# Layer 0's cross-attention attends with still values and sums by ones; the rotation of layer 1's keys goes from GpSimd to VectorE

## The chip, the cores and the metric

One core of one Trainium2 chip runs the whole program in a single launch. A core has TensorE (matrix products, 128 x 128, results to PSUM), VectorE (DVE), ScalarE (ACT), GpSimd (POOL) and SyncE (SP, which issues DMAs). The engines run side by side and meet only at semaphores; each runs its own instructions in order. Times are device microseconds (us) of the core; the metric is the median time of an execution.

## The reference

A decoder of four layers, each with self-attention, cross-attention to a context and a feed-forward part, every one followed by a residual and a layer norm. x has 16 blocks of 128 tokens and 256 features, the context as many. All arithmetic is f32. What matters here is the second of the twelve parts, layer 0's cross-attention (12 heads of 64):

```python
kv_in = layernorm(tab_x, tab_g, tab_b)
q = layernorm(layernorm(x, vid_g, vid_b) @ Wq, q_g, q_b)
k = layernorm(kv_in @ Wk, k_g, k_b)
v = kv_in @ Wv
q, k, v = (split(q) * scale, split(k), split(v))      # 12 heads of 64
sim = jnp.einsum('bhid,bhjd->bhij', q, k)
attn = jax.nn.softmax(sim, axis=-1)
out = jnp.einsum('bhij,bhjd->bhid', attn, v)
out = out.transpose(0, 2, 1, 3).reshape(x.shape[0], x.shape[1], INNER)
return out @ Wo + bo
```

and, from layer 1's cross-attention, the rotation of the keys, which the kernel makes two stages earlier than it needs them, in the stage of layer 1's self-attention (a gated convolution):

```python
k = proj(key, Wk, bk, Lk)
k = apply_rope(k, k_cos, k_sin)     # [x1 * c - x2 * s, x1 * s + x2 * c]
```

## The kernel before

The program is a chain of stages. Within a stage every engine has a list of instructions written out by hand, and waits on counting semaphores; between stages all engines meet.

**Layer 0's cross-attention** (`l0_xattn`) treats the 16 blocks in 16 turns. All 768 = 12 x 64 inner features of a block are held as two halves of 384, six heads each; a head pair (j = 0, 1) lies on the lower and upper 64 partitions. A turn n does the scores and the attention of block n, the projections of block n + 1, the input norms of blocks n + 2 and n + 3, and the output of block n - 1. In a turn TensorE does, in this order: scores for the row maxima (`scores(1)`, `scores(0)`, L1245), the transposes of block n - 1's attended rows (`turn_out`, L1236), the query projection (L1230), the turned maxima (L1251), input transposes (L1224), output projection of block n - 1 (L1280), the scores again, turned so that the keys lie on partitions, with the maxima subtracted by a product (L1258, L1261), the key projection (L1230), the transposes of the normalised queries `qn`, the attend products (L1270), the transposes of block n - 1's result into `XT` (`turn_back`, L1286), those of the normalised keys `kn`, and the value projection.

The attend product of a head takes the exponentials `Pr` (keys on partitions, queries as columns) as weights and streams the values, 64 columns and one column of ones that makes the sum of the row. So the result has queries on partitions, and a row's sum is one number on its partition. VectorE then inverts 12 sums (`rinv`, L1476), multiplies (`on`, L1479), and TensorE must transpose `on` six times and ScalarE copy it (`oT`, L1388) before the output projection can use it.

VectorE's order in a turn: two `maximum` (L1471), moments and normalisation of the next block's queries (`wide_moments`, `wide`), input moments, residual and norm of block n - 1, moments and normalisation of the next keys (`wide(n + 1, 1)`, L1456, giving `kn`), `normalise(n)`, and `keys(n + 1)` (L1463), which scales the six transposed key tiles into `kT`, first the three of half 1, then those of half 0; the next turn's `scores` wait for these. The result of a turn's attend products lies in `pS[0]`, which `scores(0)` of the next turn overwrites.

Nobody reads the `XT` that this stage writes: the feed-forward stage behind it starts from `X` and writes `XT` anew.

**Layer 1's convolution stage** (`l1_attn`) treats the tokens in four groups of 512. Per group and per quarter m of the 512 inner features: TensorE projects (L1898), ScalarE stores (`inputs`, L1949) and makes the first tap, VectorE adds three taps (`convolve`, L2009), ScalarE applies SiLU (L1963); TensorE makes the gates (L1908), ScalarE their sigmoid (L1970), VectorE the product `yT` (`products`, L2021), TensorE the output (L1922), and VectorE and GpSimd the norm (`tail`). Beside it the keys of layer 1 (`core.keys1`, 2 x 2048 elements per partition) are rotated in four chunks of 1024: VectorE swaps partners by a shuffle (`turn_keys`, L2025, two chunks ahead of group 0, one between groups 0 and 1, one behind group 1), and GpSimd multiplies by the cosines, multiplies the swapped ones by the sines, and adds (L1877 to L1879).

Of the kernel before, what the change touches and what calls it, by code (L numbers as in the profile page):

```python
# [16 lines left out]
P = 128  # L17
NB = 16
# [1034 lines left out]
def l0_xattn(core, a):  # L1053
# [6 lines left out]
    VX = DHX + 1  # L1060
    LAST = NB - 1
    with Stage(core, "x0") as s:
# [16 lines left out]
        qn, kn, on = (s.sb(n, [P, INNER]) for n in ("qn", "kn", "on"))  # L1079
        qT, kT, oT = (s.sb(n, [P, KI, P]) for n in ("qT", "kT", "oT"))  # L1080
        V = s.sb("V", [P, H, VX])
# [5 lines left out]
        rinv = s.sb("rinv", [P, 2, H // 2])  # L1087
# [4 lines left out]
        pO = pS[0]  # L1092
        pI = pS[1][:, 0, :].rearrange("p (k n) -> p k n", k=2 * KD)
        pX = pS[1][:, 1, 0:D].rearrange("p (k n) -> p k n", k=KD)
        y = pT[:, 0, 0:D]

        CLEARED = 5
# [17 lines left out]
        o_ready, o_inverted, on_ready = s.sem("o_ready"), s.sem("o_inverted"), s.sem("on_ready")  # L1115
        onT_ready, oT_stored = s.sem("onT_ready"), s.sem("oT_stored")
# [3 lines left out]
        xT_ready, xT_stored = s.sem("xT_ready"), s.sem("xT_stored")  # L1120
# [96 lines left out]
        def _(pe):  # L1217
# [59 lines left out]
            def output(b):  # L1277
                pe.wait_ge(oT_stored, b + 1)
# [3 lines left out]

            def turn_back(b):
                pe.wait_ge(xn_ready, b + 1)
                for k in range(KD):
                    ins = pe.transpose(pX[:, k, :], xn[:, bass.ts(k, P)], core.ident[:])  # L1286
                ins.then_inc(xT_ready, 1)
# [3399 lines left out]
```

## Time and profile before

| | |
|---|---|
| median of 3 runs | 2604.66 us (2603.99 to 2605.37) |
| the profiled execution's own time | 2604.75 us |
| its span, first to last instruction | 2602.9 us |
| granted TensorE clock, mean over the span | 0.947 |
| layer 0's cross-attention, about | 141 to 488 us |
| layer 1's convolution stage, about | 592 to 726 us |

The page of the profile gives busy times by engine, the timeline gives single instructions or runs of equal ones with their start and length, the windows give busy shares and granted clock of stretches. PE is TensorE's matrix products, PEld its weight loads. One f32 product shows as two passes of PE in such rows. The granted clock is a share of 2.4 GHz; 0.50 is 1.2 GHz. Names are those of the program with a letter for the stage (x_ for a cross-attention, a_ for layer 1's convolution stage).

### The profile page before, as it was taken

The numbers are of one execution on the slowest core, as the hardware profiler recorded it, in microseconds if no ns is written. First come the engines' busy times: TensorE is split into PE (matmuls) and PEld (weight loads), VectorE is DVE, ScalarE is ACT, GpSimd is POOL, SyncE is SP. The second block draws the span as 40 slices with busy tenths as digits, with TensorE's granted clock in tenths as the row PEclk, the third lists the DMA queues.
The fourth block names the chain that finished last, engine by engine and source line by source line (L and its number), as shares of the span: only waits on it lengthen the run. The fifth ranks groups of instructions, "written<-read, shape, count | busy, mean of one in ns | idle before, by whom it ended". The sixth has DMA issues, their size and how long they took to land. (4 is left out here: it accounts for less than half of the span.)

```text
span 2602.9 us, 48661 instructions
## 1 busy us (share of the span) xinstructions
PE 2283.5 (88%) x18360; PEld 1789.3 (69%) x18369; DVE 1313.6 (50%) x2768; ACT 908.1 (35%) x1591; POOL 708.3 (27%) x1096
## 2 busy tenths in 40 slices
PE   8869999787989999999979988977976889599992
PEld 4647777453567465899968866735865768399992
DVE  4566666698668421111167755553147787511114
ACT  2233333484346301111122225522225667122223
POOL 1722222235223100222212211211324532133332
PEclk9889999898989999999999989988988999799996
DMA  7500000100020100788610002013620000399994
GB/s 282 187 1 1 0 0 1 26 2 0 1 92 2 52 0 1 295 315 315 232 49 0 0 25 73 2 51 89 180 62 5 2 2 3 108 325 326 324 327 138
DMA packets 162729, 253.57 MB, mean 97 GB/s; under 512 B 17296, under 2 KB 123537, under 8 KB 162321
## 3 DMA queue, kind: packets, MB, share of 16 engines
q1 hardware_dynamic: 153360, 230.42, 25.7%
q0 software_dynamic: 9216, 21.06, 3.0%
q8 instruction: 103, 1.69, 0.3%
q14 instruction: 50, 0.40, 0.1%
HBM read 219.79 MB, written 31.13 MB: 96 GB/s over the span
## 5 line engine op out<-in xcount | busy, mean ns | idle before, releaser
L3510 PE MATMUL te_pU<-te_xsT,te_wu 128*128 128x128 f32 x1952 | 233.7, 277 | 1.5 <-DVE te_xsT L3603 1.5
L3510 PEld LDWEIGHTS te_pU<-te_xsT,te_wu 128*128 128x128 f32 x1952 | 231.3, 193 | 5.2 <-issue 2.1
L3531 PE MATMUL te_pY<-te_wd,te_hT 128*128 128x256 f32 x976 | 220.8, 379 | 0.0
L3531 PEld LDWEIGHTS te_pY<-te_wd,te_hT 128*128 128x128 f32 x976 | 180.7, 190 | 22.0
L1230 PE MATMUL x_pB<-early,x_xlT 128*128 128x384 f32 x376 | 133.4, 499 | 1.7 <-ACT x_xlT L1362 1.7
L3560 ACT ACTIVATE te_hT<-te_pU 128x512 f32<-128x512 f32 x78 | 46.6, 597 | 235.0 <-PE te_pU L3510 235.0
L2541 DVE TENSOR_REDUCE x_mx<-x_pR 128x8 f32<-128x1024 f32 x64 | 78.3, 1223 | 78.0 <-PE x_pR L2301 78.0
L3584 DVE COPY te_ys<-te_pY 128x256 f32<-128x256 f32 x61 | 25.9, 425 | 162.8 <-PE te_pY L3531 162.8
L3579 DVE TENSOR_TENSOR te_hT<-te_pU,te_sg 128x512 f32<-128x512 f32 x44 | 30.4, 692 | 147.5 <-ACT te_sg L3558 147.5
L2541 DVE TENSOR_REDUCE a_mx<-a_pR 128x8 f32<-128x1024 f32 x64 | 78.3, 1224 | 44.2 <-PE a_pR L2301 44.2
L3558 ACT ACTIVATE te_sg<-te_pG 128x512 f32<-128x512 f32 x44 | 26.3, 597 | 210.2 <-PE te_pG L3510 210.2
L1230 PEld LDWEIGHTS x_pB<-early,x_xlT 128*128 128x128 f32 x376 | 68.8, 193 | 43.1 <-issue 4.3
L2301 PE MATMUL a_pR<-a_kx,a_qx 32*128 32x128 f32 x1024 | 74.7, 282 | 24.7 <-DVE a_qx L2548 18.6
L2445 ACT ACTIVATE x_Pr<-x_pT 128x1024 f32<-128x1024 f32 x64 | 65.6, 1025 | 79.8 <-PE x_pT L2306 79.8
L3581 DVE COPY te_xsT<-te_pT 128x256 f32<-128x256 f32 x61 | 25.7, 421 | 130.8 <-PE te_pT L3504 130.8
L2301 PEld LDWEIGHTS a_pR<-a_kx,a_qx 32*128 32x128 f32 x1024 | 63.4, 186 | 38.1 <-issue 23.9
L3472 POOL COPY te_home<-moe_home 128x1 uint32 (+1 forms) x61 | 11.1, 181 | 286.7 <-DVE te_ys L3584 286.7
L3510 PE MATMUL te_pG<-te_xsT,te_wg 128*128 128x128 f32 x704 | 85.8, 275 | 0.0
L2301 PEld LDWEIGHTS x_pR<-x_kx,x_qx 32*128 32x128 f32 x1024 | 66.5, 196 | 25.0 <-issue 21.7
L2301 PE MATMUL x_pR<-x_kx,x_qx 32*128 32x128 f32 x1024 | 79.0, 294 | 4.3 <-DVE x_qx L2548 3.7
L3510 PEld LDWEIGHTS te_pG<-te_xsT,te_wg 128*128 128x128 f32 x704 | 82.1, 192 | 0.0
L3462 POOL DMA_INDIRECT te_xs<-xs_slots,te_token x65 | 64.9, 998 | 51.9 <-POOL te_token L3459 51.9
(669 smaller groups left out, 5624.8 us busy)
## 6 DMA issues: line engine op xcount, KB each, us to landing
te_wu<-in_L_ffn_w_upT SPq DMA_DIRECT2D x39, 1024.0 KB, 5.9
te_wd<-in_L_ffn_w_downT SPq DMA_DIRECT2D x39, 1024.0 KB, 5.8
te_wu<-in_L_ffn_up SPq DMA_DIRECT2D x22, 1024.0 KB, 4.9
te_wg<-in_L_ffn_gate SPq DMA_DIRECT2D x22, 1024.0 KB, 6.9
te_wd<-in_L_ffn_down SPq DMA_DIRECT2D x22, 1024.0 KB, 7.6
moe_first<-in_L_ffn_W SPq DMA_DIRECT2D x8, 1024.0 KB, 8.5
xs_slots<-zeros SPq DMA_DIRECT2D x1, 5120.0 KB, 15.6
ys_slots<-zeros SPq DMA_DIRECT2D x1, 5120.0 KB, 28.9
```

The costliest lines, as they stand in the source:

```text
L1230: ins = pe.matmul(to[:, n, 0:HALF], xlT[t][:, src + k, :], w[:, k, bass.ts(n, HALF)], start=(k == 0), stop=(k == KD - 1))
L2301: return pe.matmul(pR[:, j, c, :], qx[b % 4][g, c, :], kx[b % 4][g, c, :], start=mask is None, stop=mask is None or c == SLOTS16 - 1)
L2445: ins = act.activation(Pr[b % 2][half][:], pT[:], ACT.Exp, scale=SCALE)
L2541: dve.tensor_reduce(out, pR[:].rearrange("p j (i t) n -> p (j i) t n", i=PAIR), AX.X, ALU.max).then_inc(mx_ready[half], 1)
L3462: pool.indirect_dma_start(xs[u][:], None, core.XS, bass.IndirectOffsetOnAxis(token[u][:, 0:1], 0)).then_inc(x_loaded[u], 16)
L3510: ins = pe.matmul(out[g][:, m, :], w[:, k, bass.ts(PER * g + m, P)], xsT[:, k, :], start=(k == 0), stop=(k == KD - 1))
L3531: ins = pe.matmul(pY[u][:, 0, :], hT[:, k, :], wd[u][:, k, :], start=(k == 0), stop=(k == KH - 1))
L3558: act.activation(sg[g][:], pG[g][:], act_fn).then_inc(g_done, 1)
L3560: act.activation(hT[:, PER * g:PER * (g + 1), :], pU[g][:], act_fn).then_inc(h_done, 1)
L3579: dve.tensor_tensor(hT[:, PER * g:PER * (g + 1), :], pU[g][:], sg[g][:], ALU.mult).then_inc(h_done, 1)
L3581: dve.tensor_copy(xsT[:], pT[:, 0:KD, :]).then_inc(xT_stored, 1)
L3584: dve.tensor_copy(ys[u][:], pY[u][:, 0, :]).then_inc(y_used, 1)
```

## The change

In `l0_xattn` the roles in the attend product are swapped: the values of a head, 128 x 64, are the weights, and the 128 columns of `Pr` are streamed. The result has features on partitions and queries as columns; the two heads of a pair go to the lower and upper 64 partitions of one PSUM bank, `pS[half][:, 0]`. That is the order in which the output projection wants it, so `turn_out` with its six transposes and ScalarE's copy is gone. A row's sum now lies along columns, so it is made by a product of its own: ones of 128 x 64 as weights, the 384 columns of three heads streamed, giving the sum of each column on all 64 partitions, in `pS[half][:, 1]`. VectorE inverts these 384 columns and multiplies, once for each half, straight into `oT`. `scores(1)` of the next turn now waits for both. `invert(n, 0)` stands ahead of `wide(n + 1, 1)`, the rest behind it.

`turn_back` (transposes of xn, copy to `XT`) and the memset of the ones column in V are dropped.

In `l1_attn` all four steps of a chunk's rotation are VectorE's: 16 steps, two behind each of the first three products of groups 1 to 3. GpSimd's three are gone.

```diff
-        rinv = s.sb("rinv", [P, 2, H // 2])
+        rinv = s.sb("rinv", [P, 2, HALF])
...
-                pool.memset(V[:], 1.0).then_inc(cleared, 1)
...
                 for c in range(THIRD):
                     for j in range(2):
                         h = 2 * (THIRD * half + c) + j
-                        o = h % (H // 2) * VX
-                        ins = pe.matmul(pO[:, half, o:o + VX], Pr[:, half, j, c, :], V[:, h, :], start=True, stop=True)
-                return ins
-
-            def turn_out(b):
-                pe.wait_ge(on_ready, b + 1)
-                wide_transposes(on).then_inc(onT_ready, 1)
+                        pe.matmul(pS[half][rows(j), 0, bass.ts(c, P)], V[:, h, :], Pr[:, half, j, c, :], start=True, stop=True)
+                for j in range(2):
+                    ins = pe.matmul(pS[half][rows(j), 1, 0:HALF], core.ones[:, 0:DHX],
+                                    Pr[:, half, j, :, :].rearrange("p c n -> p (c n)"), start=True, stop=True)
+                ins.then_inc(o_ready[half], 1)
...
             def output(b):
-                pe.wait_ge(oT_stored, b + 1)
+                pe.wait_ge(oT_ready, 2 * b + 2)
...
                 if one:
-                    if isinstance(n, int) and n == 1:
-                        pe.wait_ge(e_done[1], n)
-                    else:
-                        pe.wait_ge(xT_stored, n - 1)
+                    pe.wait_ge(oT_ready, 2 * n)
                 scores(1)
                 pe.wait_ge(kT_stored, 2 * n + 2)
-                if one:
-                    pe.wait_ge(on_ready, n)
                 scores(0)
-                if one:
-                    turn_out(n - 1)
...
-                attend(1).then_inc(o_ready, 1)
-                if one:
-                    turn_back(n - 1)
+                attend(1)
...
-            def normalise(n):
-                dve.wait_ge(o_ready, n + 1)
-                ov = pO[:, :, 0:H // 2 * VX].rearrange("p a (h d) -> p a h d", d=VX)
-                dve.reciprocal(rinv[:], ov[:, :, :, DHX]).then_inc(o_inverted, 1)
-                dve.wait_ge(o_inverted, n + 1)
-                for j in range(2):
-                    ins = dve.tensor_tensor(on[:, bass.ts(j, HALF)].rearrange("p (h d) -> p h d", d=DHX),
-                                            ov[:, j, :, 0:DHX],
-                                            rinv[:, j, :].unsqueeze(2).to_broadcast([P, H // 2, DHX]), ALU.mult)
-                ins.then_inc(on_ready, 1)
+            def invert(n, half):
+                dve.wait_ge(o_ready[half], n + 1)
+                dve.reciprocal(rinv[:, half, :], pS[half][:, 1, 0:HALF]).then_inc(o_inverted, 1)
+
+            def normalise(n, half):
+                dve.wait_ge(o_inverted, 2 * n + half + 1)
+                dve.tensor_tensor(oT[:, THIRD * half:THIRD * (half + 1), :].rearrange("p c n -> p (c n)"),
+                                  pS[half][:, 0, 0:HALF], rinv[:, half, :], ALU.mult).then_inc(oT_ready, 1)
...
                 if more1:
                     wide_moments(n + 1, 1)
+                invert(n, 0)
+                if more1:
                     wide(n + 1, 1)
-                normalise(n)
+                normalise(n, 0)
+                invert(n, 1)
+                normalise(n, 1)
                 if more1:
                     keys(n + 1)
...
-            for i in range(len(chunks)):
-                rotate(i)
...
                     dve.tensor_tensor(yT[:, m, :], xc[g % 2][:, m, :], gt[:, m, :], ALU.mult).then_inc(yT_ready, 1)
+                    if g and m < KI - 1:
+                        for i in range(2):
+                            rotate(2 * ((KI - 1) * (g - 1) + m) + i)
...
+                if step == 0:
+                    ins = dve.stream_shuffle(out=turned[:], in_=k, mask=swap)
+                elif step == 1:
+                    ins = dve.tensor_tensor(over_blocks(k), over_blocks(k), table(core.x1.cosT), ALU.mult)
+                elif step == 2:
+                    ins = dve.tensor_tensor(over_blocks(turned[:]), over_blocks(turned[:]), table(core.x1.sinT), ALU.mult)
+                else:
+                    ins = dve.tensor_tensor(k, k, turned[:], ALU.add)
+                rotations.then(ins)
...
+            core.x1.wait(dve)
```

## Rows read from the trace of the kernel before

**Rows 1.** The page's first part: busy time of each engine over the span

```profile
PE 2283.5 (88%) x18360; PEld 1789.3 (69%) x18369; DVE 1313.6 (50%) x2768; ACT 908.1 (35%) x1591; POOL 708.3 (27%) x1096
```

**Rows 2.** Windows: length, busy PE, PEld, DVE, ACT, POOL, granted clock, DMA

```profile
316.00:336.00 20.00, 20.00 (x149) 15.29 (x148) 13.62 (x35) 7.74 (x17) 5.50 (x15) 1.00 0.00 0
...
467.00:469.00 2.00, 2.00 (x6) 1.62 (x5) 0.00 (x0) 0.00 (x0) 0.00 (x0) 0.52 0.00 0
```

**Rows 3.** Timeline of one turn of layer 0's cross-attention: start, length, engine

```profile
316.25 2.79 PE L1270 MATMUL x_pS<-x_V,x_Pr 128*128 128x65 f32 x24
...
318.04 1.08 DVE L1456 TENSOR_SCALAR x_kn<-x_pB,x_mvw,x_rw 128x768 f32<-128x768 f32 x1 [0.66 <-POOL x_rw L1155]
...
319.26 0.85 PE L1236 MATMUL x_pT<-ident,x_kn 128*128 128x128 f32 x6
...
319.35 1.02 DVE L1479 TENSOR_TENSOR x_on<-x_pS,x_rinv 128x384 f32<-128x384 f32 x2
...
319.94 2.75 PE L1230 MATMUL x_pB<-early,x_xlT 128*128 128x384 f32 x8
...
320.29 2.00 DVE L1463 TENSOR_SCALAR x_kT<-x_pT,early 128x128 f32<-128x128 f32 x6
...
322.62 1.61 PE L1245 MATMUL x_pS<-x_kT,x_qT 64*128 64x128 f32 x24
...
324.16 0.88 PE L1236 MATMUL x_pT<-ident,x_on 128*128 128x128 f32 x6
...
324.87 2.75 PE L1230 MATMUL x_pB<-early,x_xlT 128*128 128x384 f32 x8
...
336.17 2.79 PE L1270 MATMUL x_pS<-x_V,x_Pr 128*128 128x65 f32 x24
```

**Rows 4.** One line of the next stage, two RECIPROCALs: min/median/max ns, forms

```profile
L1777 DVE RECIPROCAL f_inv<-f_am x2: 165/203/241, 489.2 to 494.1; 128x2 f32<-128x2 f32 x1, 128x14 f32<-128x14 f32 x1
```

**Rows 5.** Groups by line and form on DVE: RECIPROCAL of PSUM operands

```profile
L2573 DVE RECIPROCAL x_R<-x_pO 128x16 f32<-128x16 f32 x32 | 8.0, 249 | 4.8 <-PE x_pO L2343 4.8
...
L1476 DVE RECIPROCAL x_rinv<-x_pS 128x12 f32<-128x12 f32 x16 | 3.7, 232 | 2.5 <-PE x_pS L1270 2.5
```

**Rows 6.** Timeline of layer 1's cross-attention: products in 32-column tiles

```profile
780.52 1.08 PE L2336 MATMUL x_pO<-x_Pr,x_V 128*32 128x128 f32 x32
```

**Rows 7.** Timeline of the stage's last turn and end

```profile
466.08 4.47 PE L1280 MATMUL x_pT<-early,x_oT 128*128 128x256 f32 x12
...
472.69 2.86 PE L1270 MATMUL x_pS<-x_V,x_Pr 128*128 128x65 f32 x24
...
479.06 5.34 PE L1280 MATMUL x_pT<-early,x_oT 128*128 128x256 f32 x12 [0.89 <-ACT x_oT L1388]
...
487.54 0.37 ACT L1393 COPY XT<-x_pS 128x256 f32<-128x256 f32 x1 [8.53 <-PE x_pS L1286]
```

**Rows 8.** One line of layer 1's convolution: min/median/max ns

```profile
L2009 DVE SCALAR_TENSOR_TENSOR a_cv<-a_xi,early,a_cv x48: 737/752/2868, 597.6 to 675.5; 128x512 f32<-128x512 f32 x48
```

**Rows 9.** Timeline of layer 1's convolution stage

```profile
597.63 19.14 DVE L2009 SCALAR_TENSOR_TENSOR a_cv<-a_xi,early,a_cv 128x512 f32<-128x512 f32 x12 [2.89 <-ACT a_cv L1956]
...
603.32 0.78 ACT L1949 ACTIVATE a_xi<-a_pA,early,ternary_mean 128x512 f32<-128x512 f32 x1 [0.18 <-PE a_pA L1898]
...
617.58 8.65 PE L1908 MATMUL a_pD<-a_xc,early 128*128 128x512 f32 x16 [8.12 <-ACT a_xc L1963]
...
643.39 1.78 PE L1922 MATMUL a_y<-early,a_yT 128*128 128x256 f32 x7 [0.91 <-DVE a_yT L2021]
...
692.23 0.69 DVE L2021 TENSOR_TENSOR a_yT<-a_xc,a_gt 128x512 f32<-128x512 f32 x1 [2.74 <-ACT a_gt L1970]
```

**Rows 10.** Groups on POOL, 592 to 645 us: one of the rotation's three lines

```profile
L1878 POOL TENSOR_TENSOR a_turned<-a_turned,early 128x1024 f32<-128x1024 f32 x4 | 10.7, 2685 | 0.0
```

**Rows 11.** Groups on DVE: a shuffle and a product of 1024 elements

```profile
L2554 DVE TENSOR_TENSOR a_Pr<-a_Pr,early 128x1024 f32<-128x1024 f32 x32 | 39.0, 1218 | 0.0
...
L2025 DVE STREAM_SHUFFLE a_turned<-early 128x1024 f32<-128x1024 f32 x4 | 5.1, 1298 | 0.0
```

More of the change, by code:

```diff
@@ L1059, in l0_xattn @@
     THIRD = KI // 2
-    VX = DHX + 1
     LAST = NB - 1
@@ L1078, in l0_xattn @@
         xlT = [s.sb(f"xlT{i}", [P, 2 * KD, P]) for i in range(2)]
-        qn, kn, on = (s.sb(n, [P, INNER]) for n in ("qn", "kn", "on"))
+        qn, kn = (s.sb(n, [P, INNER]) for n in ("qn", "kn"))
         qT, kT, oT = (s.sb(n, [P, KI, P]) for n in ("qT", "kT", "oT"))
-        V = s.sb("V", [P, H, VX])
+        V = s.sb("V", [P, H, DHX])
         mx = [s.sb(f"mx{i}", [P, 2, THIRD]) for i in range(2)]
@@ L1114, in l0_xattn @@
         e_done = [s.sem(f"e_done{i}") for i in range(2)]
-        o_ready, o_inverted, on_ready = s.sem("o_ready"), s.sem("o_inverted"), s.sem("on_ready")
-        onT_ready, oT_stored = s.sem("onT_ready"), s.sem("oT_stored")
+        o_ready = [s.sem(f"o_ready{i}") for i in range(2)]
+        o_inverted, oT_ready = s.sem("o_inverted"), s.sem("oT_ready")
         y_ready, r_ready, xres_ready = s.sem("y_ready"), s.sem("r_ready"), s.sem("xres_ready")
@@ L1281, in output @@
                 ins.then_inc(y_ready, 1)
[L1283 to L1287, printed above, removed]
             def turn(n, u, one, more1, more2, more3):
@@ L1374, in value @@
                 act.wait_ge(v_ready, b + 1)
-                act.copy(V[:, :, 0:DHX].rearrange("p (a h) d -> p a h d", a=2),
+                act.copy(V[:].rearrange("p (a h) d -> p a h d", a=2),
                          pB[:, :, 0:HALF].rearrange("p a (h d) -> p a h d", d=DHX)).then_inc(V_stored, 1)
@@ L1384, in exponentials @@
                 act.activation(Pr[:, half, :, :, :], thirds(pS[half]), ACT.Exp, scale=SCALE).then_inc(e_done[half], 1)
-            def turn_out(b):
-                act.wait_ge(onT_ready, b + 1)
-                act.copy(oT[:].rearrange("p (a c) n -> p a c n", a=2), thirds(pT)).then_inc(oT_stored, 1)
-            def turn_back(b):
-                act.wait_ge(xT_ready, b + 1)
-                hold(act, core)
-                act.copy(core.XT[:, :, bass.ts(b, P)], pX).then_inc(xT_stored, 1)
             def turn(n, u, one, more1, more2, more3):
-                if one:
-                    turn_out(n - 1)
                 maxima(n, 1)
@@ L1405, in turn @@
                     query(n + 1)
-                if one:
-                    turn_back(n - 1)
                 if more1:
@@ L1416, in _ @@
             every_turn(act, turn)
-            turn_out(LAST)
-            turn_back(LAST)
         @block.vector
@@ L1864, in _ @@
             early.wait(pool)
-            rotations = Steps(pool, ksteps, 100)
-            rotations.turn(0)
-            def over_blocks(t, n):
-                return t[:, n[0], n[1]].rearrange("p (b n) -> p b n", n=P)
-            def table(t):
-                return t[:].unsqueeze(1).to_broadcast([P, HALF // P, P])
-            def rotate(i):
-                pool.wait_ge(shuffled, i + 1)
-                k, k2 = over_blocks(core.keys1, chunks[i]), over_blocks(turned, chunks[i])
-                pool.tensor_tensor(k, k, table(core.x1.cosT), ALU.mult)
-                rotations.then(pool.tensor_tensor(k2, k2, table(core.x1.sinT), ALU.mult))
-                rotations.then(pool.tensor_tensor(k, k, k2, ALU.add))
             tail.pool_residual(pool, 0, b_out[:])
             tail.pool_residual(pool, 1, b_out[:])
-            for i in range(len(chunks)):
-                rotate(i)
             for p in range(2 * NG):
@@ L2021, in products, with over_blocks, table, rotate @@
                     dve.tensor_tensor(yT[:, m, :], xc[g % 2][:, m, :], gt[:, m, :], ALU.mult).then_inc(yT_ready, 1)
-            def turn_keys(i):
-                t, here = chunks[i]
-                dve.stream_shuffle(out=turned[:, t, here], in_=core.keys1[:, t, here], mask=swap).then_inc(shuffled, 1)
-            turn_keys(0)
-            turn_keys(1)
+                    if g and m < KI - 1:
+                        for i in range(2):
+                            rotate(2 * ((KI - 1) * (g - 1) + m) + i)
+            rotations = Steps(dve, ksteps, 4 * len(chunks))
+            rotations.turn(0)
+            def over_blocks(t):
+                return t.rearrange("p (b n) -> p b n", n=P)
+            def table(t):
+                return t[:].unsqueeze(1).to_broadcast([P, HALF // P, P])
+            def rotate(n):
+                if n >= 4 * len(chunks):
+                    return
+                i, step = divmod(n, 4)
+                k = core.keys1[:, chunks[i][0], chunks[i][1]]
+                if step == 0:
[8 more added lines that the diff above has]
+            core.x1.wait(dve)
             for m in range(KI):
                 convolve(0, m)
-            turn_keys(2)
             for m in range(KI):
                 convolve(1, m)
-            turn_keys(3)
             for g in range(NG):
```

12 lines of the change are left out of this document (3 added, 9 removed).

## The prediction

> **What bounds the kernel now.** I read the page first: TensorE is busy 88% of the span [rows 1]. That is an average over a dozen stages, so I went to the windows of the stage that changes. From 196 to 436 us every window of 20 us looks like the one shown [rows 2]: PE busy for all of it at full clock, VectorE 13.6 us, ScalarE 7.7, GpSimd 5.5. Then the timeline of one turn [rows 3]. It is exactly periodic: the attend products start at 316.25 and again at 336.17, so a turn takes 19.92 us. TensorE never rests in it. VectorE has 6 us to spare, but not everywhere: the key normalisation (`wide`, L1456, 318.04 to 319.12) is followed at 319.26 by the TensorE transposes of it, which start as soon as the attend products are out of the way. There VectorE is just in time. The reader is to see that this stretch, attend, kn, transposes, kT, scores, has next to no slack on either engine, and the change puts its new VectorE work precisely there.
>
> **Part 1: the attend products.** Before, 12 products are 24 TensorE passes of 65 columns in 2.79 us, 116 ns each [rows 3]; a pass of 128x128 weights costs that whatever few columns it streams. After, values stand still: 24 passes of 128 columns in 64-column tiles, two heads side by side. The trace has no 64-column tile. Its nearest row is the 32-column tiles of layer 1, 32 passes in 1.08 us, or 34 ns each with four side by side [rows 6]; two side by side would be 68 ns, so 1.6 us a turn. New are the sums by ones: four products of 384 columns, 8 passes. A pass of 384 columns takes 2.75/8 = 0.344 us [rows 3]; two side by side, 1.4 us a turn. Together 3.0 us, where 2.79 stood: TensorE gains nothing here. Bounds: if tiles didn't overlap, 2.8 + 2.75 = 5.5 us. Within one half the second tile runs a pass behind the first, so a half's result is complete about 0.8 + 3 x 0.344 = 1.8 us after its start.
>
> The Trainium skill (TensorEngine Tiling (Array Packing), Key Properties) says that changing the tiling mode drains the array; that would add two drains a turn, for which no row here gives a price.
>
> **Part 2: what goes.** The six transposes of `on` (324.16 to 324.87, 0.7 us of TensorE a turn) and the two of xn, with ScalarE's two copies; ScalarE has room, so its copies are worth nothing but at the stage's end. The memset of V lies beside other work. If nothing else changed, the turn would be some 0.7 us shorter, 11 us over the stage.
>
> **Part 3: the reciprocal.** Before, one RECIPROCAL of 12 elements per partition, 0.23 us. After, every column sum stands on all rows of its head, so there are two RECIPROCALs of 384 elements. The trace has none so wide, so I want its slope. In one line of the next stage, the same tile's 2 and 14 elements take 165 and 241 ns [rows 4]: 6.33 ns an element, where an ordinary product of 1024 elements takes 1218 ns, 1.2 ns an element [rows 11]. From PSUM, 12 take 232 and 16 take 249 ns [rows 5], 4.25 ns an element. So a width of 384 costs 165 + 382 x 6.33 = 2.58 us by the first, 249 + 368 x 4.25 = 1.81 us by the second. I take 2.58, since it spans more elements and gives 228 and 254 ns for the PSUM pair, within 5 ns. The lower end is 1.81; an ordinary rate of 0.55 us (half of the 1.02 for two passes of 384 [rows 3]) I leave to the rivals.
>
> The Trainium skill (VectorE: DVE Perf Modes, First, the fixed hardware budget) says that reciprocal is an iterated divide with a repeat count of 8. Its chip overview gives VectorE 0.96 GHz (Trainium Kernel Development and Optimization, NeuronCore Architecture); an estimate by both is 384 x 8 / 0.96 = 3.2 us, which the sum below would turn into about 2679 us. The trace agrees that an element takes several cycles, with 6.33 ns.
>
> **The new turn**, in the times of [rows 3], attend at 316.25:
> - `invert(n, 0)` starts when half 0 is complete and seen, 316.25 + 1.8 + 0.2 (taken for the last pass to drain and be signalled) = 318.25, ends 320.83. Queued behind it on VectorE are `wide` of the keys, the rest of normalise, and `keys`.
> - `wide` (1.08): 320.88 to 321.96; was 319.12.
> - TensorE's kn transposes start 322.1; were 319.26. TensorE, done with attend at about 319.5, idles 2.5 us. The value projection follows, 322.8 to 325.5.
> - VectorE meanwhile: normalise(0) 0.55 to 322.55, invert(1) to 325.2, normalise(1) to 325.8. Only then `keys` (0.33 each, L1463): half 1 ready 326.85, half 0 at 327.85.
> - `scores(1)` 326.95, was 322.62; TensorE idles again 1.4 us. `scores(0)` 327.95 to 328.72.
> - The query projection starts 328.75; was 324.87. This is +3.9 us, with the 0.7 us of Part 2 already taken off.
> From there to the next attend nothing changes: GpSimd's maxima parts follow the scores by as much as before and all other waits have microseconds of cover. So a turn is 23.8 us instead of 19.92. VectorE would then be busy 13.6 - 0.2 + 5.2 = 18.6 of 23.8: it isn't full, its order is the bound. There are 15 such intervals: **+58 us**. Each 0.1 us of the reciprocal is 0.2 us a turn, 3 us in all.
>
> The stage's end: attend at 472.69, output at 479.06 [rows 7]. After: 472.69 + 2.0 + two reciprocals and two products with gaps (6.5) = 481.2, +2.1. The XT copy of 0.37 us that closed the stage is gone: together **+1.7**.
>
> The clock: in the last turn, transposes and two idle gaps of under 1 us each from 463.2 on were enough for the granted clock to read 0.52 in the window at 467 [rows 2], half of 2.4 GHz, and the 12 output passes took 4.47 us instead of 2.75 [rows 7]. The new idle 2.5 us plus transposes looks alike. It lands on the value projection, 1.7 us longer, of which 1.4 is covered by the wait for keys; 0.3 a turn in half the turns: **+2**, bounds 0 and the rival below.
>
> **Part 4: key rotation on VectorE.** In layer 1's convolution stage GpSimd's 12 passes over 1024 elements (2.69 us each, [rows 10]) run beside VectorE's taps, of which a group's 12 take 19.14 us (1.6 each) though the line's median is 0.75 [rows 8, 9]. TensorE waits 8.12 us for the last and starts its gates at 617.58. Without GpSimd beside them, group 0's taps end at about 607, so ScalarE sets the pace: its first store of group 1 ends 604.1 [rows 9], then four SiLUs (0.7) and three more stores (0.8) in turn, with bank waits, to about 610.1. The gates start 7.4 us sooner. Without the long idle before them they also start at full clock: the 16 passes of 512 columns took 8.65 us [rows 9], where 512/384 of 0.344 is 0.46 each, 7.3 us; I take 1.5 for it. Another 0.9 is the outputs of group 0 no longer waiting for VectorE [rows 9]. That is -9.8.
> The rotation itself costs VectorE one shuffle (1.30) and three products (1.22) [rows 11] for each of four chunks, 19.8 us, two steps between products of groups 1 to 3; the four shuffles it did before, 5.2 us, go. In group 1 TensorE is behind enough gates to cover it. In group 2 VectorE, by the same working through, starts its products at about 675.3 after the moments (an estimate), and 4 x 0.7 + 3 x 2.5 = 10.3 us later yT is complete, at 685.6; TensorE, moved up by 9.8, has got through gates, transposes and the outputs' first passes at 683.4 and waits 2.2 us (before, the last yT was there at 692.92, about when it was needed [rows 9]). In group 3 the steps fit between gates. Sum **-7.6**; bounds -4 (the wait lowers the clock) and -10.
>
> **Sum** against the profiled execution's own 2604.75 us (span 2602.9, and 0.1 above the median 2604.66): +58 + 1.7 + 2 - 7.6 = +54, so **2659 us**.
>
> **Rivals.**
> *The reciprocal runs at the rate of a product* (0.55 us at 384). For: nothing shown is wide, and small ones may hide a start-up. Against: 2 to 14 elements already differ by 76 ns. Then kn ends at 319.9, scores start at 323.4, and a turn stays within 0.1 us of 19.92; the end gains 2.4; with Part 4, 2595 us. It decides from below about 0.9 us for 384 elements; above, the kernel is slower. This is the case of the other sign.
> *The 64-column tiles don't overlap.* For: no row has them. Against: the 32-column ones do [rows 6]. Half 0 is complete 0.9 us later, and the chain with it: +14, 2673 us.
> *The reciprocal is steeper at width.* If the fixed part of an instruction hides the first elements' work, the slope between 2 and 14 is too flat; a quarter more, 3.2 us, gives +1.2 a turn, 18 in all and 1 at the end: 2679 us. This is also what the Trainium skill's repeat count would give (VectorE: DVE Perf Modes, First, the fixed hardware budget). Against: 2, 12, 14 and 16 elements lie on one line.
> *The clock falls onto uncovered work* (scores, query projection) in each turn. For: two gaps a turn, 2.5 and 1.4 us. Against: between them TensorE works. At 1.7 us a turn: +26, less the 2 already in, 2683 us.
> *The reciprocal follows the flatter PSUM slope*, 1.81 us: a turn 1.5 us shorter, 2635 us. This I count as the forecast's own lower part.
>
> **How the numbers follow.** Forecast with both its slopes 0.58; steeper 0.10; clock 0.11; tiles 0.08; fast reciprocal 0.09; and 0.04 that shortfalls cancel within 0.2%, which is what a measurement here tells from no change. Faster 0.09, same 0.04, slower 0.87. The range, 2630 to 2688, runs from below the flat slope to above the clock rival, leaving out the fast reciprocal and mixtures of the high ones.
>
> **What would show it.** RECIPROCAL 128x384 at 2.6 us (1.8; 0.55); the turn 23.8 us between attend groups; kn transposes waiting for VectorE about 2.5 us and scores waiting for `x_kT`; attend groups in about 3 us; granted clock mostly 1.00 in the stage; the convolution taps at 0.75 and gates from 18 us, not 25, after the stage's start. The prediction is wrong if the wide reciprocal is short, for all else hangs on it.

## The result, and the profile after

The changed kernel takes 2654.2 us (median of 4 runs, 2651.5 to 2655.7) against 2605.0 us for the kernel before (4 runs): a ratio of 1.0184, 95% interval 1.0169 to 1.0200, so it is 1.8% slower. The prediction said slower and 2659 us, 4.8 us above the median. The profiled execution has a span of 2649.7 us, 46.8 more than before. In the experiments below two executions were far slower than all others of the same kernel (3153 us of e_order_twice, 9151 us of the kernel before) and are left out of the ratios.

First the groups of instructions by line, on VectorE, from 170 to 540 us of the changed kernel. Columns: line, engine, operation, tiles and shapes, count, busy time and mean length of one, idle time ahead of them.

```profile
L1436 DVE RECIPROCAL x_rinv<-x_pS 128x384 f32<-128x384 f32 x32 | 81.7, 2553 | 9.3 <-PE x_pS L1266 9.3
L1424 DVE TENSOR_SCALAR x_kT<-x_pT,early 128x128 f32<-128x128 f32 x90 | 30.0, 402 | 0.0
...
L1440 DVE TENSOR_TENSOR x_oT<-x_pS,x_rinv 128x384 f32<-128x384 f32 x32 | 17.7, 553 | 0.6
```

One inversion of 384 sums takes 2553 ns, where the product of 384 elements takes 553. They are now VectorE's longest group in the stage, though each sum in them stands on 64 rows and is inverted 64 times.

Next TensorE's waits from 176 to 540 us after: who waited for whom, us in total, how often, the longest.

```profile
PE x_pT L1231 <- DVE x_kn L1417: 35.2, 15, 2.3
PE x_pS L1240 <- DVE x_kT L1424: 5.8, 6, 1.0
PE x_pT L1273 <- DVE x_oT L1440: 5.0, 1, 5.0
```

Before, the same two waits were 0.2 us in all and nothing. The transposes of the keys wait 2.3 us in each of the 15 turns; the scores wait for the scaled keys in only 6. The timeline of one turn says why it is only 6 (start, length, and in brackets the idle time before and what ended it); it answers to [rows 3].

```profile
316.22 0.88 PE L1264 MATMUL x_pS<-x_Pr,x_V 128*64 128x128 f32 x12
...
316.93 0.81 PE L1266 MATMUL x_pS<-x_Pr,ones 128*64 128x384 f32 x4
317.57 0.83 PE L1264 MATMUL x_pS<-x_Pr,x_V 128*64 128x128 f32 x12
...
322.07 4.44 PE L1225 MATMUL x_pB<-early,x_xlT 128*128 128x384 f32 x8
...
326.44 1.61 PE L1240 MATMUL x_pS<-x_kT,x_qT 64*128 64x128 f32 x24
327.98 2.85 PE L1225 MATMUL x_pB<-early,x_xlT 128*128 128x384 f32 x8
...
338.88 0.82 PE L1231 MATMUL x_pT<-ident,x_qn 128*128 128x128 f32 x6
339.63 0.88 PE L1264 MATMUL x_pS<-x_Pr,x_V 128*64 128x128 f32 x12
```

The attend is as short as worked out (12 passes in 0.71 us and four passes of 384 columns in 0.64, from start to start). The value projection at 322.07 takes 4.44 us where it took 2.75 [rows 3]: it runs behind TensorE's idle time, at the lower level of the clock for most of its length. So it, not the keys, ends last ahead of the scores. The windows of this turn (length, busy time and count of PE, PEld, DVE, ACT, POOL, granted clock, DMA share, GB/s) show the clock:

```profile
316.22:322.00 5.78, 3.43 (x39) 2.44 (x39) 5.06 (x8) 2.20 (x6) 1.24 (x2) 1.00 0.00 0
322.00:326.40 4.40, 4.40 (x11) 2.12 (x8) 4.37 (x8) 0.00 (x0) 0.00 (x0) 0.61 0.00 0
326.40:331.00 4.60, 4.60 (x36) 3.16 (x36) 2.24 (x4) 0.88 (x2) 1.50 (x8) 1.00 0.00 0
```

Of the 15 intervals from attend to attend 8 are 23.3 to 23.4 us, with the slow projection, and six 22.5 to 22.9, with one of 2.75 us, in which the scores start 9.6 us after the attend and not 10.2. TensorE's idle time of 2.35 us is the same in both kinds; what decides whether the clock falls behind it was not tried. The last interval, in which TensorE has less to do, is 19.6 us (before 17.4). The first attend starts at 176.89 and the last at 520.48, 343.6 us apart; before, 295.9. The stage costs 47.7 us in its turns. At its end the last output starts 7.8 us after its attend, before 6.4 [rows 7]; the next stage's first work on VectorE starts 16.75 us after it, before 15.54, so the end costs 1.2.

Of layer 1's convolution stage two places, on PE and DVE. The first answers to the start of [rows 9], the second is the third group's output:

```profile
641.55 16.62 PE L1842 MATMUL a_pA<-XT,early 128*128 128x512 f32 x32 [0.80 <-PEq L285]
647.10 9.18 DVE L1953 SCALAR_TENSOR_TENSOR a_cv<-a_xi,early,a_cv 128x512 f32<-128x512 f32 x12 [7.11 <-ACT a_cv L1900]
...
731.47 1.55 PE L1866 MATMUL a_y<-early,a_yT 128*128 128x256 f32 x6
...
734.69 0.69 DVE L1965 TENSOR_TENSOR a_yT<-a_xc,a_gt 128x512 f32<-128x512 f32 x1
735.44 7.57 PE L1866 MATMUL a_y<-early,a_yT 128*128 128x256 f32 x26 [2.42 <-DVE a_yT L1965]
```

Twelve taps take 9.18 us without GpSimd's multiplications beside them, where they took 19.14 [rows 9]. They were not slowed evenly: before, the five taps that ran while GpSimd was at work took 2.72 to 2.84 us each, about as long as its passes (2.35 to 2.79), and the seven behind them 0.75. The gates start 18.1 us after the stage's start instead of 25.4. In the third group the rotation makes the last product late: TensorE waits 2.42 us, and its 26 passes then take 7.57 us. At full clock 32 of them take 7.07. The stage is 128.4 us long, before 133.9.

### The profile page after: what moved, and what is told of

It is laid out like the page before. It is cut to its first block and busy times, and to the rows that moved or that the text cites. A ratio compares the mean times of both kernels' runs of the same rounds, so it can differ in the third digit from the quotient of the medians.

```text
span 2649.7 us, 48611 instructions
## 1 busy us (share of the span) xinstructions
PE 2290.4 (86%) x18360; PEld 1772.3 (67%) x18369; DVE 1381.3 (52%) x2796; ACT 888.9 (34%) x1559; POOL 676.1 (26%) x1083
## 3 DMA queue, kind: packets, MB, share of 16 engines
q1 hardware_dynamic: 153360, 230.42, 25.3%
## 5 line engine op out<-in xcount | busy, mean ns | idle before, releaser
L1225 PE MATMUL x_pB<-early,x_xlT 128*128 128x384 f32 x376 | 148.2, 543 | 1.7 <-ACT x_xlT L1338 1.7
L1225 PEld LDWEIGHTS x_pB<-early,x_xlT 128*128 128x128 f32 x376 | 75.1, 210 | 51.8 <-issue 17.2
L2265 PE MATMUL a_pR<-a_kx,a_qx 32*128 32x128 f32 x1024 | 74.7, 282 | 24.7 <-DVE a_qx L2512 18.6
L1436 DVE RECIPROCAL x_rinv<-x_pS 128x384 f32<-128x384 f32 x32 | 81.7, 2553 | 9.3 <-PE x_pS L1266 9.3
```

The lines of the kernel that those rows point to most:

```text
L1225: ins = pe.matmul(to[:, n, 0:HALF], xlT[t][:, src + k, :], w[:, k, bass.ts(n, HALF)], start=(k == 0), stop=(k == KD - 1))
L1436: dve.reciprocal(rinv[:, half, :], pS[half][:, 1, 0:HALF]).then_inc(o_inverted, 1)
L2265: return pe.matmul(pR[:, j, c, :], qx[b % 4][g, c, :], kx[b % 4][g, c, :], start=mask is None, stop=mask is None or c == SLOTS16 - 1)
```

## The experiments

The time of each stands beside that of the kernel before, measured with it on the same chip. To compare the stages I take the distance from the first to the last pass of the attend: 298.5 us before (176.8 to 475.3), 345.5 after (176.9 to 522.4).

**e_xattn_only**: the new layer 0 cross-attention, the rotation left where it was.

```diff
 l0_xattn: as in the changed kernel
 l1_attn:  as in the kernel before (rotate(i) on GpSimd, turn_keys(i) on VectorE)
```

> The new layer 0 cross-attention with the key rotation left on GpSimd as before. Theory (two separate parts, one that costs 3 us a turn and one that gives back 5.5 us in layer 1's convolution stage): the cross-attention stage ends 49 us later as in the changed kernel, and nothing in layer 1 gives any of it back, so about 2605 + 49 + 2 = 2656 to 2661 us, that is 3 to 7 us above the changed kernel. Rival (the cross-attention's loss is all there is and the rotation gave nothing, since the 5.5 us were only the clock of that one execution): the same as the changed kernel, 2652 to 2655.

Measured: 2657.7 us against 2604.7, ratio 1.0200 (1.0185 to 1.0216). The attend's distance is 347.5 us, and the convolution stage 134.0 us again, within the theory's range. Two separate parts, as the theory had it.

**e_rot_only**: the other half alone.

```diff
 l0_xattn: as in the kernel before
 l1_attn:  as in the changed kernel
```

> The layer 0 cross-attention of before, the key rotation on VectorE. Theory: the first convolution taps run free of GpSimd's multiplications, the first gate projection starts about 7 us earlier and the third output's wait gives 2 to 4 us back, so 3 to 6 us less than before: 2599 to 2602. Rival (the rotation steps between the last products only move the work, and the gain in the changed kernel came from a different phase of the clock): within 2 us of before, 2603 to 2607.

Measured: 2600.9 us, ratio 0.9981 (0.9972 to 0.9990). The rotation's move is worth 3.8 us in all: its stage is 127.9 us, 6.1 shorter, and the start of the next stage gives 2.1 of it back (below, under "Not foreseen"). Its trace has the same 2.42 us wait in the third group, with 7.43 us of passes behind it, and a granted clock of 0.83 from 680 to 690 us:

```profile
680.50 1.56 PE L1904 MATMUL a_y<-early,a_yT 128*128 128x256 f32 x6
684.48 7.43 PE L1904 MATMUL a_y<-early,a_yT 128*128 128x256 f32 x26 [2.42 <-DVE a_yT L2003]
```

**e_no_recip**: the length of the inversion, and nothing else. The kernel leaves the inversion out: the results are multiplied by their sums.

```diff
-    dve.reciprocal(rinv[:, half, :], pS[half][:, 1, 0:HALF])
+    dve.tensor_copy(rinv[:, half, :], pS[half][:, 1, 0:HALF])
```

> The changed kernel with each of the two inversions of 384 sums a turn replaced by a plain copy of the sums; this leaves the inversion out, so the values are multiplied by their sums rather than divided. Waits, order and tiles stay. Theory (the inversion's 2.55 us, twice a turn on VectorE ahead of the scaled keys, is the whole loss): a copy of 384 elements takes 0.4 to 0.6 us, so the chain is 4 us shorter, and TensorE's value projection then ends last, as in the kernel before; turn 19.9 to 20.4 us in place of 23.1, and 2601 to 2612 us in all. Rival 1 (the normalised keys stand behind the first inversion's wait in VectorE's order, and that order costs the time): most of the loss stays, since the wait for the first half's sums stays: turn above 21.5, over 2630. Rival 2 (the attend in 64-column tiles and its sums of 384 columns on TensorE cost the time): the same, turn above 22.

Measured: 2598.8 us, ratio 0.9976 (0.9966 to 0.9985); the attend's distance 296.2 us. That is a little below the theory's range (2601 to 2612) and far from the rivals' 2630. Orders, waits, tiles and sums by ones are those of the changed kernel. Its timeline of the same stretch, PE and DVE:

```profile
318.05 0.88 PE L1264 MATMUL x_pS<-x_Pr,x_V 128*64 128x128 f32 x12
...
319.61 0.56 DVE L1436 COPY x_rinv<-x_pS 128x384 f32<-128x384 f32 x1 [0.54 <-PE x_pS L1266]
...
320.09 1.07 DVE L1417 TENSOR_SCALAR x_kn<-x_pB,x_mvw,x_rw 128x768 f32<-128x768 f32 x1
321.07 0.55 DVE L1440 TENSOR_TENSOR x_oT<-x_pS,x_rinv 128x384 f32<-128x384 f32 x1
321.30 0.85 PE L1231 MATMUL x_pT<-ident,x_kn 128*128 128x128 f32 x6 [0.44 <-DVE x_kn L1417]
...
321.99 2.75 PE L1225 MATMUL x_pB<-early,x_xlT 128*128 128x384 f32 x8
```

With 0.56 us in place of 2.55, TensorE waits 0.44 us for the keys instead of 2.3, the value projection keeps its clock (2.75 us), and the turn is 19.8 us. Both rivals, the order of VectorE's queue and the 64-column tiles, are out: they are all still there. The reciprocal, with what its waiting does to the clock, is the whole loss.

**e_ln_exp**: the same inverse from an engine that is idle there.

```diff
+    act.activation(rinv[:, half, :], pS[half][:, 1, 0:HALF], ACT.Ln)
+    act.activation(rinv[:, half, :], rinv[:, half, :], ACT.Exp, scale=-1.0)
-    dve.reciprocal(rinv[:, half, :], pS[half][:, 1, 0:HALF])
```

> The changed kernel with each inversion done on ScalarE as exp(-ln(sum)), in order behind the scaled queries. ScalarE does nothing between those and the values' copy. Theory (only the length of the inversions on VectorE matters): two activations of 384 elements take about 0.5 us each, the first half's inverse comes 1.1 us after its sums in place of 2.6, the second 1 us behind it, and the turn falls from 23.1 to 20 to 20.5 us: 2600 to 2612 us. Rival (the functions of logarithm and exponential come from different tables, and the load of a table stands in each turn): two to four loads a turn of more than 1 us each on the chain, turn of 23 or more, 2650 or more, with loads of tables in ScalarE's rows.

Measured: 2702.9 us, ratio 1.0373 (1.0357 to 1.0389); attend's distance 397.5 us. The rival was right. ScalarE's groups by line, for the whole program:

```profile
L1352 ACT ACT_TABLE_LOAD x32 | 41.1, 1283 | 0.6
L1354 ACT ACT_TABLE_LOAD x32 | 41.1, 1283 | 0.6
...
L1354 ACT ACTIVATE x_rinv<-x_rinv 128x384 f32<-128x384 f32 x32 | 16.7, 523 | 0.4
...
L1352 ACT ACTIVATE x_rinv<-x_pS 128x384 f32<-128x384 f32 x32 | 15.7, 490 | 0.4
```

The two functions take 1.0 us, as guessed, but the tables are changed before each: four loads of 1283 ns a turn. All four stand between the scaled queries and the second half's inverse. The scores come 11.2 us after the attend, behind 4.8 us in which TensorE has nothing to do, and in the turn from 310.6 us they take 2.93 us in place of 1.61 and the query projection 4.39 in place of 2.85: part of this loss is the clock. The Trainium skill (ScalarE: Activation LUTs, Table sets: the hidden batching unit) says that one set holds both functions and that a logarithm followed by an exponential needs one load. This program's trace has one ahead of every Ln and one ahead of every Exp of the pair, 64 in all, so the pair was not served from that set here; why, the runs do not show.

**e_order**: inversion behind the normalised keys.

```diff
-                invert(n, 0)
                 if more1:
                     wide(n + 1, 1)
+                invert(n, 0)
                 normalise(n, 0)
```

> The changed kernel with the first half's inversion behind the normalised keys in VectorE's order, in place of ahead of them. VectorE's work up to the scaled keys is the same 9 us. Theory (VectorE's chain ends last, the order in it is nothing): the keys' transposes and the value projection start 2 us earlier in the turn, the scores do not, and the time is within 6 us of the changed kernel's 2654: 2648 to 2660. Rival (in the turns in which TensorE's value projection runs at half clock it is this projection that ends last, so the late normalised keys cost): 5 to 12 us less, 2642 to 2649.

Measured: 2680.2 us against 2605.6, ratio 1.0289 (1.0274 to 1.0304); attend's distance 372.6 us. A miss for both theories: I had it equal or faster, and it is 26 us slower than the changed kernel. The waiting for the keys' transposes did go, and the scores come 9.9 us after the attend instead of 10.2 in most turns of the changed kernel and 9.6 in the others. But from the scores to the next attend it is then 14.8 us and not 13.2. The windows of one of its turns:

```profile
325.79:332.20 6.41, 6.25 (x47) 3.84 (x46) 5.53 (x8) 2.24 (x7) 1.25 (x2) 1.00 0.00 0
332.20:335.68 3.48, 0.00 (x1) 0.00 (x1) 3.45 (x6) 0.77 (x1) 0.00 (x0) 1.00 0.00 0
335.68:338.20 2.52, 2.52 (x24) 2.10 (x24) 1.86 (x4) 0.00 (x0) 0.28 (x2) 0.66 0.00 0
338.20:342.00 3.80, 3.80 (x14) 2.29 (x13) 1.05 (x2) 0.04 (x1) 1.30 (x7) 0.78 0.00 0
342.00:350.50 8.50, 8.50 (x66) 6.45 (x64) 6.55 (x20) 3.52 (x8) 2.75 (x5) 1.00 0.00 0
```

TensorE does nothing from 332.20 to 335.68, and what comes next is granted 0.66 and 0.78: the scores take 2.61 us in place of 1.61, the query projection 3.65 in place of 2.85. In the changed kernel the idle time lies ahead of the value projection, of whose slowness most is hidden by the wait for the keys. Here it lies ahead of work that nothing covers. This was now a theory, and the runs so far only fitted it.

**e_order_keys**: the same order, and the keys scaled on ScalarE.

```diff
 e_order, and:
-    dve.tensor_scalar(kT[:, k, :], pT[...], gqk[:, 1, k:k + 1], bqk[:, 1, k:k + 1], ALU.mult, ALU.add)
+    act.activation(kT[:, k, :], pT[...], ACT.Identity, bias=bqk[:, 1, k:k + 1], scale=gqk[:, 1, k:k + 1])
```

> The order of the run before this one, and the keys scaled and biased on ScalarE (six activations of 128 columns, 0.37 us each), which has nothing to do then, in place of VectorE. Theory (the two inversions and the scaled keys stand one behind the other on VectorE): the keys are ready before the second half is normalised, the scores wait for that alone, 1.3 to 2 us sooner a turn, and 16 turns give 20 to 30 us back: 2624 to 2635 us. Rival (ScalarE's queue or TensorE's clock takes it up): 2642 or more.

Measured: 2650.7 us, ratio 1.0173 (1.0158 to 1.0188); distance 351.4 us. The theory (2624 to 2635) missed. The scores come 9.0 us after the attend, 0.9 sooner than in e_order where the theory wanted 1.3 to 2, and TensorE waits 2.7 us ahead of them, so the clock takes its share: the number is the rival's (2642 or more).

**e_order_twice and e_order_keys_twice**: the test of the clock. More work, put into the wait.

```diff
 e_order (and e_order_keys), and:
+                    project(wv, KD, 1 - u)
                     project(wv, KD, 1 - u).then_inc(v_ready, 1)
```

> The run with the inversion behind the normalised keys, with the value projection done twice over, one behind the other into the same place: 2.75 us more of matmuls a turn, put where TensorE waits 3.5 us with nothing to do. Theory (that run's extra loss is the clock: behind the idle wait the scores and the query projection run at 0.66 and 0.78 of the full clock): with the wait filled the clock stays full, the turn falls from 24.7 to 23.1 us though more is computed, and the time from 2680 to 2650 to 2660. Rival (the loss is VectorE's chain alone, or a wait that the clock only goes with): the same 2680 or more.

> The same doubled value projection in the run with the keys scaled on ScalarE. Its scores come 9.0 us after the attend's start, and TensorE has 2.7 us of nothing to do ahead of them. Theory (clock): the turn falls from 23.3 to 22.2 us and the time from 2651 to 2633 to 2640. Rival: 2651 or more, since the second projection ends at about 9.1 us and lies ahead of the scores.

Measured: 2654.5 us for the first, ratio to before 1.0178 (1.0159 to 1.0196), and 2631.9 us for the second, 1.0098 (1.0082 to 1.0113). The distances are 347.3 us, 25.3 less than without the second projection, and 330.7, 20.7 less. The first lies in the range that the clock theory gave (2650 to 2660); the second is 1 us below its range (2633 to 2640), with the turn of 22.2 us that it gave. Both are far from the rival's numbers. The windows of a turn of e_order_twice:

```profile
317.62:321.20 3.58, 3.49 (x39) 2.49 (x39) 2.73 (x6) 2.20 (x6) 1.24 (x2) 1.00 0.00 0
321.20:326.50 5.30, 5.30 (x18) 2.87 (x16) 5.23 (x5) 0.00 (x0) 0.00 (x0) 1.00 0.00 0
326.50:329.30 2.80, 1.81 (x25) 1.49 (x24) 2.72 (x7) 0.80 (x1) 0.00 (x0) 1.00 0.00 0
```

VectorE's chain is the same to 0.1 us (327.51, the scores' start, is 9.9 after the attend). All that changed is that TensorE computes the values a second time and is idle for 0.97 us where it was for 3.55. The granted clock stays at 1.00 and the turn is 23.21 us where it was 24.7. So 25 of the 75 us that e_order lost were the clock.

**e_keys_act**: the keys on ScalarE, with VectorE's order of the changed kernel.

> The changed kernel with the keys scaled on ScalarE alone; VectorE's order stays (inversion ahead of the normalised keys), so TensorE's idle time lies ahead of the value projection and not behind it. Theory: the second half is normalised 8.5 us after the attend's start, the value projection ends at 8.6 us at full clock and at 10.3 us at half, so the turns with the clock down gain nothing and the others 1.5 us: 2632 to 2650 us, less than the 2651 of the run with both edits only if the clock holds. Rival (VectorE's keys are the whole of what stands between): 2624 to 2630.

Measured: 2644.5 us, ratio 1.0149 (1.0134 to 1.0165); distance 342.5 us. Within the range, and faster than e_order_keys, whose scores come 1.2 us sooner after the attend. In its timeline the value projection, 315.98 to 320.28, takes 4.37 us, and the scores follow it at once: 10.2 us after the attend, exactly as in the changed kernel. In such a turn the shorter chain of VectorE gains nothing. In four of the 15 turns the projection keeps its clock, and there the scores come 8.7 us after the attend and the turn is 21.8 to 21.9 us.

**e_rot_moved**: before's cross-attention, the rotation's 16 steps spread another way over the four groups' products.

```diff
-                    if g and m < KI - 1:
-                        for i in range(2):
-                            rotate(2 * ((KI - 1) * (g - 1) + m) + i)
+            STEPS = ((0, 0, 2, 3), (2, 2, 2, 0), (1, 0, 0, 0), (2, 2, 0, 0))
+                    for i in range(STEPS[g][m]):
+                        rotate(sum(sum(row) for row in STEPS[:g]) + sum(STEPS[g][:m]) + i)
```

> The cross-attention of before, the key rotation on VectorE, but its 16 steps spread as 5, 6, 1 and 4 over the products of the four groups in place of 0, 6, 6 and 4. In the profile of the rotation alone VectorE has 7.2 us of idle time around the first group's products, and TensorE waits 2.4 us for the third group's last product and then runs its output at a lower clock. Theory (that wait is made by the six steps): the wait and 1.7 us of clock go, 3 to 4 us less than the rotation alone: 2596 to 2599. Rival (the wait is for the convolution's taps, or ScalarE's): the same 2601.

Measured: 2597.9 us against 2605.6, ratio 0.9971 (0.9959 to 0.9982). TensorE's timeline of the third group:

```profile
683.88 7.07 PE L1904 MATMUL a_y<-early,a_yT 128*128 128x256 f32 x32
690.79 13.90 PE L1890 MATMUL a_pD<-a_xc,early 128*128 128x512 f32 x32
```

The wait is gone and all 32 passes take 7.07 us. From the gates' start at 612.06 to the next stage's first projection at 718.36 it is 106.3 us; in e_rot_only (608.69 to 718.86) 110.2. The trace shows the 3.9 us; the two intervals of the times still overlap.

**e_dead_rot_moved**: and the transposes that nothing reads taken out of before's cross-attention.

```diff
 e_rot_moved, and in l0_xattn:
-                if one:
-                    turn_back(n - 1)
```

> As the run before this one, and in the cross-attention of before the last transposes of each block, which nothing reads, are gone (TensorE's two transposes, ScalarE's copy and the two waits), with everything else of it as before. Theory (these sit beside the longer work of TensorE and ScalarE, 0.3 us a turn at most, and 1 us at the stage's end): 0 to 5 us less than the run before this one: 2592 to 2599. Rival (their absence only changes where TensorE idles and what clock it gets): within 1 us of it or slower.

Measured: 2598.3 us, ratio 0.9973 (0.9962 to 0.9984); distance 299.3 us, before 298.5. Nothing is gained. The theory allowed for that (0 to 5), and so did the rival.

**e_rot_none**: no rotation anywhere.

```diff
 e_rot_only, and:
-                    if g and m < KI - 1:
-                        for i in range(2):
-                            rotate(2 * ((KI - 1) * (g - 1) + m) + i)
```

> The cross-attention of before, and no rotation of layer 1's keys at all: GpSimd's and VectorE's steps are both gone, which leaves out the rotation. It bounds what any place for it can give. Theory (the rotation on VectorE costs 4 us at the third group, and with its steps spread nothing more): 2595 to 2599 us, the same as the spread rotation within 2 us. Rival (VectorE's 20 us of rotation still cost elsewhere): 2590 or less.

Measured: 2597.6 us against 2606.0, ratio 0.9965 (0.9952 to 0.9979). With the rotation gone altogether the kernel is no faster than with its steps well placed; from the gates' start to the next stage 105.8 us (607.88 to 713.71), 0.5 less than in e_rot_moved. Spread like that, 20 us of VectorE cost nothing that the times show. The whole stage is 121.3 us there and 124.0 in e_rot_moved, but 2.3 of these 2.8 lie ahead of the gates, in the first projections: their first 4.6 us were granted 1.00 in the one profile and 0.51 in the other.

## Why the prediction was right, point by point

**What bounds the kernel** held: VectorE's order between attend and scores had no slack, and the new work was put there. e_no_recip shows that the inversions' length alone decides. (In the last of the windows that I called alike, 416 to 436 us, VectorE has 11.5 us and not 13.6; nothing rests on it.)

**Part 1** (TensorE gains nothing) held: 3.0 us were forecast, and 2.8 measured. From start to start, twelve passes of 128 columns take 0.71, 59 ns each where I took 68, and four of 384 take 0.64, 0.16 each where I took 0.17. A half is complete 1.5 us after its start, not 1.8. The rival in which the tiles don't overlap is out.

**Part 2** was mis-sized as a gain. I took 0.7 us of transposes off the turn, and off this stretch they are: from the scores to the query projection it is 1.54 us after (326.44 to 327.98) and 2.25 before. But from there to the next attend it is 11.65 us where it was 11.30, so half of the gain is lost again. About 0.2 of it lies at the turned maxima, which now wait for GpSimd; my sentence that all other waits have microseconds of cover was wrong there. Another 0.1 lies at the entry to the attend: it starts 0.75 us after the transposes of the queries where it was 0.65, in every turn. The transposes of xn gained nothing: in e_dead_rot_moved TensorE waits 0.22 us in their place for VectorE's normalised keys, and the turn is 19.9 us as before.

**Part 3**: the reciprocal was sized right, 2.58 us forecast from 2 and 14 elements, 2.55 measured on 384. The flat slope (1.81), the steep one (3.2) and the rate of a product (0.55) are out. The Trainium skill's repeat count (VectorE: DVE Perf Modes, First, the fixed hardware budget), which the estimate turned into 3.2 us, is too high by a quarter at this width: 2553 less 165 ns over 382 elements is 6.25 ns an element.

**The new turn**: forecast 23.8 us, measured 22.9 on average, so +47.7 us for the 15 intervals and not +58. The part from the scores to the next attend was sized right (13.1 us forecast, 13.2 to 13.3 measured); all of the error lies ahead of the scores, which I had 10.7 us after the attend and which come at 10.2 or 9.6. The terms that were off are small ones added up along the chain: the first half is complete 0.3 us sooner and seen 0.15 us sooner, and VectorE's next instruction starts some 0.1 us before the end of the one ahead of it at four of five joints, where I had gaps. The second inversion began at 321.62, forecast 322.6. That each 0.1 us of the reciprocal weighs 0.2 us a turn was not measured by itself; the two ends fit it: with 4.0 us less of inversion a turn the attend's distance is 49.3 us shorter, 3.3 a turn, and then other work ends last.

**The clock** was seen in the right place and taken too light. The value projection did run at half in more than half the turns, and 0.5 us of it stuck out in 8 of them, about 4 us where I had 2. The rival (the clock falls onto uncovered work in each turn, 2683 us) was wrong for this kernel and right for one edit beside it: e_order moves the idle time from ahead of the covered projection to ahead of the scores and lands at 2680.

**The end** cost 1.2 us, forecast 1.7: the last output starts 1.4 us later, forecast 2.1.

**Part 4** gave 5.5 us in its stage, forecast 7.6 (bounds 4 and 10). The first gates came 7.3 us sooner, forecast 7.4, and their 16 passes took the 1.5 us less that I took, though my own rows gave only 1.3 for them. The wait in the third group was 2.42 us, forecast 2.2. What I had left as a bound came in full: the wait lowers the clock, and 26 passes take 1.8 us longer than their share of 7.07.

**Not foreseen**: at the start of layer 1's cross-attention the granted clock stays at 0.50 and 0.58 in the windows from 781 to 791 us. In the same place before (737 to 747) it was 0.69 and 1.00. From the stage's first projection to its first attend it is 25.1 us, before 23.0, so this gives back 2.1 us. It is not tied to one part of the change: all the experiments' traces have 25.1 to 25.4 us there, those of either half alone among them. What brings it about was not tried.

Sum after the runs, in the spans: +47.7 + 1.2 - 5.5 + 2.1 = +45.5, and 0.4 in the feed-forward stage between the two, of 46.8. The last 0.9 us gather behind 800 us, in stages that the change doesn't touch; nothing here explains them.

**Luck**: the total lies nearer to the forecast than its terms do. The turns with their clock were 12.3 us too dear (+60 against +47.7); Part 4 had 2.1 us too much gain, and 3.4 us came in that I had not foreseen.

Neither kernel is the best of these. e_rot_moved, before's cross-attention with the rotation on VectorE in better places, is 0.3% faster than before and, by the medians of two separate measurements, 2.1% faster than the changed kernel. Even with a copy in the inversion's place the new cross-attention got no further (e_no_recip, 2598.8 us). The fast-reciprocal rival's 2595 us was 4 us too low. So there was next to nothing to win in it; at which length of the inversion it starts to lose, which I had put at 0.9 us, was not tried between 0.56 and 2.55.

## What to carry to other kernels

Count a reciprocal per element of the free dimension, not per number wanted: broadcasting the sums ahead of the inversion turned 12 elements a turn into 768, and 0.23 us into 5.1. When you must leave TensorE waiting, choose what stands behind the wait: the clock that it loses is paid by the next matmuls, and it is cheap only if something else ends later anyway; moving one instruction past another cost 26 us here by that alone. Work moved to another engine is free only in the stretches where that engine idles: look at each group's idle time, and spread the steps unevenly by it.

## What the runs showed of the hardware

- RECIPROCAL on VectorE is linear in its width from 2 elements (165 ns) to 384 (2553 ns), 6.25 ns an element, from PSUM as from SBUF; a copy or a product of 384 takes 0.55 to 0.56 us.
- More work can be faster: 2.75 us of matmuls computed over again in each turn took 26 us off e_order, since the granted clock stayed at full (2.4 GHz) in place of 0.66 and 0.78 behind an idle time of 3.5 us. Behind the idle 0.97 us that was left, it did not fall.
- Matmuls in 64-column tiles on both halves of the array overlap: 59 ns a pass of 128 columns and 0.16 us a pass of 384, where a pass of 384 by itself takes 0.335, from start to start. Going from tiles of 128 to tiles of 64 columns the attend starts 0.10 us later behind the same transposes than before; whether that is the change of tiles was not tried, and the way back is hidden by the wait for the keys.
- ScalarE loaded its table before every Ln and every Exp that alternate, 1283 ns each time.
- While GpSimd's passes over 1024 elements ran (2.35 to 2.79 us each), a tap of VectorE lasted 2.72 to 2.84 us in place of 0.75: it took as long as the pass beside it, and seven taps behind them were not slowed at all. Taking the passes away gave 4 us in all, though VectorE took on 15 us of work for it (16 steps of about 1.24 us, less four shuffles of 1.30).
